# Linear attention plus ternary feed-forward on 8 cores: twelve row tiles turned on TensorE instead of by DMA, and weight loads, output projection and W2 sums moved

## The reference

```python
xn = layernorm(x)
# attention, 16 heads, feature size 16, value size 64
q, k, v = xn @ Wq.T, xn @ Wk.T, xn @ Wv.T
qf, kf = taylor_exp(q), taylor_exp(k)      # [1, x/2, x(x)x/(4 sqrt 2)], 273 features
y = tril(qf @ kf.T) @ v
y = y * rsqrt(mean(y*y, -1) + 1e-5) * g_weight
attn = y @ Wo.T
# feed-forward with weights in {-1, 0, 1}
t(w) = clip(round(w / mean(|w|)), -1, 1)
h = gelu(xn @ t(W1).T + b1)                # 4096 wide
out = x + attn + h @ t(W2).T + b2
```

## Time and profile before

| | us |
|---|---|
| median of 3 runs (range) | 799.35 (797.04 to 799.82) |
| profiled execution | 804.62 |
| span of its slowest core (core 5) | 803.1 |
| spans of the eight cores | 783.4 to 803.1 |
| busy PE / DVE / ACT / POOL on core 5 | 692.5 / 388.1 / 268.8 / 75.3 |

### The profile page before, as it was taken

How to read it: one execution, slowest core, us unless ns; L and a number is a source line. 1 busy time by engine, 2 the same in 40 slices (tenths; PEclk the granted TensorE clock), 3 DMA queues, 4 the chain that set the end, 5 groups by cost and what they waited for, 6 DMA issues and landing times.

```text
span 803.1 us, 11282 instructions; the slowest of 8 cores (783.4 to 803.1 us)
## 1 busy us (share of the span) xinstructions
PE 692.5 (86%) x3954; PEld 331.8 (41%) x3954; DVE 388.1 (48%) x636; ACT 268.8 (33%) x350; POOL 75.3 (9%) x111
## 2 busy tenths in 40 slices
PE   2734488776788888799999988999999999999997
PEld 1312244433444444344444433444444444444443
DVE  6665276747666556523311314462375356400554
ACT  3433166534777554225446454333200000000000
POOL 3002000202021000001111111110011000000000
PEclk9987699989899999899999999999999999999999
DMA  8699972445587822426566576534154577400565
GB/s 165 160 166 135 193 174 55 115 128 136 181 200 199 229 80 92 118 95 199 187 205 211 168 214 215 177 117 158 53 185 156 177 223 228 133 1 1 182 211 184
DMA packets 73926, 124.62 MB, mean 155 GB/s; under 512 B 34704, under 2 KB 40720, under 8 KB 73872
## 3 DMA queue, kind: packets, MB, share of 16 engines
q0 software_dynamic: 22896, 73.08, 32.8%
q1 hardware_dynamic: 50976, 50.82, 23.6%
HBM read 103.30 MB, written 16.78 MB: 150 GB/s over the span
## 4 chain that ended last, share of the span: by engine, by line
PE 56%; DMA 21%; DVE 9%; issue 7%; ACT 4%; SPq 2%; POOL 1%; DVEq 0%; ACTq 0%; POOLq 0%
DMA stg<-w2r 5%; PE pY L1140 5%; PE pST L1140 5%; PE pSS L1140 5%; PE pW L1140 5%; DMA xnT<-xn_tm 4%; DMA res<-res_scr 4%; PE pSS L1119 4%; PE pST L1119 4%; PE pW L915 4%; PE pY L1119 4%; PE pW L1055 4%; PE pW L1119 4%; PE pW L904 3%; DMA stg<-w1r 3%
## 5 line engine op out<-in xcount | busy, mean ns | idle before, releaser
L666 DVE TENSOR_SCALAR w1t<-stg,consts 128x2048 bf16<-128x2048 f32 (+1 forms) x18 | 21.2, 1175 | 112.3 <-DMA stg<-w1r 82.9
L845 ACT ACTIVATE stg<-stg 128x2048 f32<-128x2048 f32 x25 | 47.9, 1914 | 56.2 <-DMA stg<-w2r 56.1
L1140 PE MATMUL pST<-w2t,hT 128*128 128x512 bf16 x256 | 66.0, 379 | 0.1
L1140 PE MATMUL pSS<-w2t,hT 128*128 128x512 bf16 x256 | 66.0, 379 | 0.0
L1140 PE MATMUL pW<-w2t,hT 128*128 128x512 bf16 x256 | 66.0, 379 | 0.0
L1140 PE MATMUL pY<-w2t,hT 128*128 128x512 bf16 x256 | 66.0, 379 | 0.0
L1119 PE MATMUL pSS<-xnT,w1t 128*128 128x512 bf16 x272 | 61.5, 379 | 5.1 <-ACT hT L894 5.1
L915 PE MATMUL pW<-wv_sb,xnT 128*128 128x512 bf16 x232 | 56.6, 390 | 7.6 <-ACT vk L809 3.4
L1119 PE MATMUL pST<-xnT,w1t 128*128 128x512 bf16 x272 | 61.5, 379 | 0.0
L1119 PE MATMUL pY<-xnT,w1t 128*128 128x512 bf16 x240 | 55.9, 387 | 1.0 <-ACT hT L894 0.6
L1119 PE MATMUL pW<-xnT,w1t 128*128 128x512 bf16 x240 | 54.2, 379 | 0.0
(11 more groups left out here) (176 smaller groups left out, 988.7 us busy)
## 6 DMA issues: line engine op xcount, KB each, us to landing
stg<-w1r POOLq DMA_DIRECT2D x32, 1024.0 KB, 7.1
stg<-w2r POOLq DMA_DIRECT2D x32, 1024.0 KB, 6.1
xr<-x SPq DMA_DIRECT2D x16, 512.0 KB, 7.1
res_scr<-rst SPq DMA_DIRECT2D x16, 512.0 KB, 3.4
res<-res_scr SPq DMA_DIRECT2D x32, 256.0 KB, 4.4
xs<-x SPq DMA_DIRECT2D x32, 256.0 KB, 4.6
out<-osb SPq DMA_DIRECT2D x32, 256.0 KB, 2.8
wo_sb<-wo POOLq DMA_DIRECT2D x1, 2048.0 KB, 26.3
```

Source lines behind the costliest of these rows:

```text
L666: e.tensor_single_scalar(dst, src, cc(col + 1), ALU.is_lt).then_inc(sTA, 1)
L845: e.activation(buf, buf, AF.Abs, accum_out=cc(col)).then_inc(done, 1)
L1140: return e.matmul(out_bank(n), hT[:, j, 128 * t:128 * t + 128], w2t[8 * dh + j // 4][:, j % 4, :], start=(j == 0), stop=(j == NJ - 1))
```

## The change

Line numbers of the changed kernel differ; names are kept.

1. Tiles 4 to 15 are turned on TensorE as well. Each is a unit `("t", n)` of the rotation: eight matmuls into the pair whose turn it is, and a copy by ACT (`empty_turned`). `turned_first` and `turned_late` say in which step. The transposing DMAs of `xnT` are gone, and SP now only issues the loads of x there (`x_next`), the first three behind the arrival of the first weights.
2. The second half of Wv, Wo (in four parts) and the second half of Wq and Wk are issued by POOL behind the masks of given steps (`slot(i)`), and POOL's `qblk` copies stand ahead of other loads (`Q_BEFORE`).
3. The output projection lags three steps (`proj_out(i - 3)` from step 19), three of them are left for the up phase, and `y_within` stands ahead of it and of the side unit.
4. The tiles of W2 that are summed go to two buffers of their own, `stg2`, loaded by SP and summed by DVE between the ternary tiles (`abs_sum2`). ACT has no sums in the up phase. PSUM pairs of the up and down phases take another order.
5. W1 sums: DVE in steps 10 to 15, ACT in steps 16 to 25.

```diff
+def ln_tiles(i):
+    if i == 0:
+        return (5,)
+    if i == 1:
+        return (6, 7)
+    return (i + 6,) if i <= 9 else ()
+def turned_first(i):
+    return (i + 4,) if i in (1, 2) else (i + 5,) if 3 <= i <= 10 else ()
+def turned_late(i):
+    return {0: (4,), 2: (7,)}.get(i, ())
...
-        if i >= 18:
-            order += [("wo", i - 2)]
+        order += [("t", t) for t in turned_late(i)]
+        if i >= 19:
+            order += [("wo", i - 3)]
...
-Q_BEFORE = {("a1", 2): 2, ("a1", 4): 3, ("a1", 8): 4, ("a1", 12): 5, ("t1", 0): 6,
-            ("t1", 2): 7}
+Q_BEFORE = {("a1", 2): 3, ("a1", 6): 4, ("a1", 9): 5, ("a1", 13): 6, ("t1", 1): 7}
...
-            if t >= T_PE:
-                if t >= T_PE + 2:
-                    dXT.wait_done(e, t - T_PE - 2)
-                dXT.inc(e.dma_start(
-                    out=xnT[:, t, :, :],
-                    in_=xn_tm[:, t % 2, :].rearrange("p (b i) -> p b i", b=KD, i=128),
-                    transpose=True), t - T_PE)
...
         y_out(31)
+        dYT.wait_done(e, 31)
+        for n in range(16):
+            if n < 3:
+                res_out(13 + n)
+            if n >= 2:
+                e.wait_ge(sA2, n - 1)
+            dA2.inc(e.dma_start(
+                out=stg2[:, n % 2, :].rearrange("p (m f) -> p m f", m=4, f=512),
+                in_=w2_d[n].rearrange("m p f -> p m f")), n)
...
+        def slot(i):
+            e.wait_ge(dMK, i + 1)
+        for n in range(2):
+            slot(n)
+            e.dma_start(out=wv[:, 1, 4 * n:4 * n + 4, :],
...
         q_block(e, 1, range(4, 8), dQP)
+        for n, i in enumerate((3, 4, 5, 7)):
+            if i == 7:
+                q_block(e, 2, range(4, 8), dQP)
+            slot(i)
+            e.dma_start(out=wo[:, 2 * n:2 * n + 2, :] ...
+        slot(8)
         e.dma_start(out=wqk[:, 1, :, :], in_=wqk_d[1]).then_inc(dQK[1], 16)
...
-        for u in range(2, 12):
+        ternary1(2)
+        for u in range(3, 11):
             ternary1(u)
+            abs_sum2(2 * (u - 3))
+            abs_sum2(2 * (u - 3) + 1)
+        ternary1(11)
...
+        def empty_turned(t):
+            unit_filled(e, ("t", t))
+            e.copy(xnT[:, t, :, :].rearrange("p k f -> p (k f)"),
+                   banks(("t", t))).then_inc(aW, 1)
...
+        def turn_unit(t):
+            bank_free(e, ("t", t))
+            turn(banks(("t", t)), t).then_inc(pWU, 1)
```

More of the change, by code:

```diff
@@ L89, in unit_table @@
             order += [("vk", 0)]
+        order += [("t", t) for t in turned_first(i)]
         if i + 1 < NI:
@@ L391, in res_out @@
                                 in_=rst[:, c % 2, :]), c)
-        for t in range(4):
-            xn_out(t)
+        for t in range(3):
+            x_next(t)
         e.wait_ge(sMS, 4)
         q_raw(0)
+        for t in (3, 4):
+            x_next(t)
         for i in range(NI):
@@ L865, in sca_stream @@
             if i == 0:
+                ln_sqrt(4)
                 empty_own(0)
+            for t in turned_first(i):
+                empty_turned(t)
             if i >= 1:
@@ L877, in sca_stream @@
                 features_q(i + 1)
+            for t in turned_late(i):
+                empty_turned(t)
             if i in A1_ACT:
@@ L880, in sca_stream @@
                 abs_sum(("a1", n), C_A1 + n, sA1)
-            if side_unit(i) is not None and side_unit(i)[0] != "qk":
-                empty_side(side_unit(i))
             e.wait_ge(pYD, i + 1)
@@ L885, in sca_stream @@
                          AF.Square).then_inc(aYS, 1)
+            if side_unit(i) is not None and side_unit(i)[0] != "qk":
+                empty_side(side_unit(i))
             for t in ln_tiles(i)[1:]:
@@ L910, in proj_v @@
             hf, c = n // 16, n % 16
-            for sem in (dV0, [dV1])[hf]:
+            for sem in (dV0, dV1)[hf]:
                 e.wait_ge(sem, 16)
@@ L943, in spread_q, with turn @@
             mm.then_inc(pWU, 1)
+        def turn(dst, t):
+            e.wait_ge(sXN, t + 1)
+            for kd in range(KD):
+                mm = e.matmul(dst[:, 128 * kd:128 * kd + 128],
+                              xn_tm[:, t % 2, 128 * kd:128 * kd + 128], ident[:],
+                              start=True, stop=True)
+            return mm
+        def turn_unit(t):
+            bank_free(e, ("t", t))
+            turn(banks(("t", t)), t).then_inc(pWU, 1)
         def first(kind, o):
@@ L1049, in proj_out @@
             c = i - 16
-            bank_free(e, key)
+            if i == 30:
+                e.wait_ge(aG, 1)
+            elif i == 31:
+                e.wait_ge(dNM, 32)
+            else:
+                bank_free(e, key)
             dYT.wait_done(e, i)
@@ L1061, in ten_stream @@
         for t in range(T_PE):
-            e.wait_ge(sXN, t + 1)
-            for kd in range(KD):
-                mm = e.matmul(TURN[t][:, 128 * kd:128 * kd + 128],
-                              xn_tm[:, t % 2, 128 * kd:128 * kd + 128], ident[:],
-                              start=True, stop=True)
-            mm.then_inc(pT, 1)
+            turn(TURN[t][:], t).then_inc(pT, 1)
         first("q", 0)
@@ L1077, in ten_stream @@
                 e.wait_ge(sSU, N_SETUP)
+            for t in turned_first(i):
+                turn_unit(t)
             y_before(i)
@@ L1084, in ten_stream @@
                 spread_q(i + 1)
-            if i >= 18:
-                proj_out(i - 2)
+            for t in turned_late(i):
+                turn_unit(t)
+            y_within(i)
+            if i >= 19:
+                proj_out(i - 3)
             if side_unit(i) is not None:
```

121 lines of the change are left out of this document (60 added, 61 removed).

## The result

The changed kernel takes 777.75 us (median of 4 runs, 775.78 to 779.85) beside 796.09 of the kernel before on the same chip: a ratio of 0.976, interval 0.973 to 0.980. A first comparison gave 0.975 (0.970 to 0.980). It is faster, by 18 to 21 us and not by the 43 to 49 forecast. Both medians lie above the range of 746 to 775.

A forecast was written before the change was run, and what follows sets the result against it. TensorE was taken as the bound wherever it does not wait, so removed waits count in full. From the profiled 804.6 us: -31.3 + 14.0 - 13.0 - 7.1 - 11.2 = 756.0, range 746 to 775.

The forecast's parts named there:

- The signs: Expected marks: scores of step 4 near 65 us, step 16 near 176, up(0) near 302, 231 to down, clock 1.0.
- Steps 2 and 3: Start of the loop: without transposing DMAs, waits for xnT and qblk and cold stretches shrink, -31.3 us.
- cost nothing: Loads of Wv, Wo, Wq and Wk dealt out over steps: 0 us, since the waits elsewhere cover them.
- Rival A: Start of the kernel: bound by the loads, not by the turning; 9 us more, 765; chance 0.13.
- Twelve turning units: Tiles 4 to 15 turned on TensorE in the rotation: 1.2 us each, together +14.0 us.
- Rival B: Rotation becomes the bound: a turning unit costs 2.6 us, 17 us more, 773; chance 0.09.
- Copies ahead of loads: qblk copies issued earlier for steps 12 and 16: less waiting and cold clock, together -13.0 us.
- Rival C: qblk waits at steps 4, 12 and 16 stay, being DMA latency and not queue order: 773; chance 0.08.
- Lag of three: Step 31: the projection's y is a step older, so its wait and cold run go, -7.1 us; y_within first, 0.
- Rival E: More comes back: y_within in the gap fills some 0.4 us in 20 steps, -8 us, 748; chance 0.07.
- W2 sums: Up phase: separate buffers and sums on DVE recover 11.7 us lost, 0.5 kept back, -11.2 us.
- Rival D: Up phase: DVE's queue with W2 sums delays loads and holds TensorE; slower than before, 805 and above; chance 0.03.

The follow-up runs named there:

- `y_within` last: Changed kernel with y_within moved back behind the output projection and the side unit in every step, ScalarE's order to match: 775.37 us, ratio 0.974.

## Why the prediction was wrong

**The baseline, and chance.** The prediction said of the excess over the median that "its excess lies in the DMA waits that the change attacks, so I take the result of the sum as the new median as it is". The waits that went were core 5's own, but the answer is the slowest of eight cores, and they lie 6 to 14 us apart in the changed kernel too. Core 5 after is 4.9 under the slowest. A sum made on one core is that core's time; a term for the spread was missing. That is 4.9 of the 22.4 us.

**The signs.** Three of them do not follow from the sum. By its terms the scores of step 16 come at 172.4, not 176, up(0) at 297.0, not 302, and the stretch behind it is 232.1, not 231. Measured are 180.1, 315.1 and 232.1. The DMA engines stayed under 0.9 busy from 40 us on, as said, and the clock was all the same 0.7 and 0.8 in slices 3 and 4: it fell behind TensorE's waits (core 5: 0.55 behind 3.13 us in step 2, with the DMA engines 0.45 busy, and 0.58 behind 3.69 us in step 31, with 0.39) and not with a full DMA.

**Steps 2 and 3: the mechanism right, the size 2 us or more short.** The prediction gave -31.3 and 5.6 for five units, 25.7 net; core 5 lost 23.7 in the first profile, 20.8 in the second. Scores of step 4 came at 66.49, "near 65". The old loads beside the new turning left steps 2 and 3 at 25.9, so the gain is from turning alone, and "cost nothing" for the dealt-out loads held there. What it left out are the two waits behind the second square root, 3.13 and 1.55; behind the first the projection ran at a clock of 0.55 (3.29 us instead of 1.89). Moving the square root gave back 1.4. Rival A fell: in steps 1 to 3 VectorE, which reads x, never waited for a load of it. The Trainium skill (Advanced Engine Details and Errata, "X-Bar Transpose (TRN2)") says that transposing DMAs are as fast as regular ones. No run here sets the two transfers side by side. What this trace shows is the issue: of the twelve turnings on core 5 eight took SyncE 1.2 to 1.3 us, and four between 53 and 102 us took 2.3 to 9.4, beside 0.6 to 1.9 for the loads of x there. The 9.43 us that the prediction named came behind the copies for step 4 in SyncE's queue (81.12 and 73.01) and cannot have held them; what stood ahead put them behind GpSimd's loads.

**Twelve turning units: the size right, the reason not.** The prediction took 1.2 each; steps 5, 6, 7, 9 and 10 grew by 1.0 in the mean. It argued from the unit's matmuls and the copy ahead of it. The kernel with one matmul showed that the matmuls do not set it: the unit shifts the next values onto the scores' pair. Rival B, 2.6 each, fell.

**Steps 4, 8 and 12: a wait not foreseen.** The prediction priced the landing of the `qblk` copies and not of the two `qf` copies issued behind them. In step 4 TensorE stood 2.1 us for them and ran the projection in 3.49 instead of 1.89. Before, they landed about when the `qblk` copies did, for which TensorE stood 18.5 us, and no wait of their own shows. This is what the prediction had allowed for in words, "unless something else is late in its place", and not in its sum. Values placed ahead took back 3.2 us in three steps. The price of 5.6 us for a group of copies was an upper bound read from the scores: they land in about 2 us ahead of a large load, and one behind it in 4 to 15.

**Copies ahead of loads: right at step 11, lost at step 15.** Step 11 went from 14.8 to 7.9 us on core 5 (forecast -7.5), step 15 only from 12.1 to 9.5 (forecast -5.5). On core 5 no wait for `qblk` is left; at step 12 one for `qf` took its place, 1.7 to 4.3 us on seven cores of the first profile and on two of the second. With `y_within` late step 15 takes 5.6 to 5.8, so the rest of its term was taken by the mask. Rival C fell for steps 12 and 16: with the old queue the waits were 7 to 11 us, with the new one gone. In step 8 cores 0 and 2 have 3.3 us.

**Lag of three, "`y_within` first": the step that failed.** The prediction gave the lag -7.1 and the place of `y_within` nothing: "What `y_within` fills between `spread_q` and the side unit it takes from the cover before the next values: 0." The wait for y did go from step 31 (others of up to 2.5 us stand in steps 20 and 24 of some cores). But `y_within` waits for the mask, which VectorE makes behind whatever stands in its queue. In step 31, core 5, that is the emptying of a projection and half a ternary tile:

```profile
304.97 1.23 DVE L673 COPY rst<-pW 128x1024 f32<-128x1024 f32 x1 [2.77 <-PE pW L1121]
306.11 0.68 DVE L768 TENSOR_REDUCE consts<-ysq 128x8 f32<-128x512 bf16 x1
306.71 0.74 DVE L701 TENSOR_SCALAR w1t<-stg,consts 128x1024 bf16<-128x1024 f32 x1
307.56 1.28 DVE L704 SCALAR_TENSOR_TENSOR w1t<-stg,consts,w1t 128x1024 bf16<-128x1024 f32 x1
308.76 0.68 DVE L739 TENSOR_TENSOR Am<-Am,tril 128x1024 bf16<-128x1024 bf16 x1
```

TensorE stood 3.69 us for it, and the projection behind took 5.30 us instead of 3.61, most of it at a clock of 0.58. In step 15 it is a W1 sum that stands there, in step 17 the scaling of Wo. The early place was a new wait at the head of the projections. With it late in step 31, the stretch is 5.6 us on every core against core 5's 12.1 before: that is the forecast's -7.1, short by 0.6. Together with steps 15 and 17 the place cost about 10 us, nearly half of the miss, and without it the time is inside the range. Rival E priced the early place as a gain of 8. A gain there is, 0.2 to 1.3 us in nine steps, 5 in all (steps 5 to 10, 24, 25 and 27 of `y_within` last), but the three waits outweigh it. The lag of three itself was not tried apart from the pairs; 5.4 us on all cores with it and 6.9 to 12.3 with a lag of two, `y_within` last in both, speaks for it. That steps 16 to 30 did not lose the 3.46 us of the third projection is seen in them: step 18, which has no projection now, lost 3.6, and on core 5 steps 17 and 19 took 2.8 and 2.4 more, step 17 by the mask, step 19 by waits for the state (0.97) and for ScalarE (0.72) and a projection in 4.27 us. The rest, 0.2 to 0.4 us in each of several later steps, was not traced.

**W2 sums: right.** The terms give 232.1 us from first up to first down product, and 232.1 were measured on six of eight cores; alone on the kernel before, 228.6 against a bare 228.2. VectorE's 16 sums take 2.28 us each, as reckoned. It did wait for W2, up to 3.9 us, and no up product was late for it. In the whole the part is worth the slowest core's loss, 1.1%. Rival D fell.

## What to carry to other kernels

Read the instruction that a moved piece waits for, and the queue of the engine that makes it, at each place it will stand; a short piece (0.4 us) put ahead of a long one (3.6 us) can cost 5. The best place of such a piece may differ from step to step, and then the places add up. In a rotation of few bank pairs price a unit by the pair that it pushes the next one onto, not by its own length; and when a sum is made on the slowest core of one execution, add back the spread that the new kernel will have. Issue small copies ahead of a large load, by however little: half a microsecond behind it cost the copy 3 us and more.

## What was unexpected of the hardware

An eighth of the matmuls in the turning units changed steps of 8 to 10 us by 0.1 us or less, and four of these steps (5, 6, 9 and 10) repeat to 0.03 us in variants that do not touch them, on three chips: away from DMA waits the schedule is set to that grain. Six small copies issued by SyncE in a row did not gain by their order: putting two ahead of four moved 2 to 3 us from one place to the other, since the one copy issued behind GpSimd's load lands in 5.1 to 8.4 us and the others in about 2.
